# One transformer layer with mixture of experts on one core: the last batch's block results summed on TensorE, in place of a store and a gather by row

## What is computed

```python
x = x + attention(layernorm(x))              # 16 heads, causal softmax, projection wo
y = layernorm(x)                             # 4096 tokens x 128
shared = gelu(y @ Wfc_s + bfc_s) @ Wproj_s + bproj_s
p = softmax(y @ Wr); topk_p, topk_i = top_k(p, 2); topk_p /= sum(topk_p)
routed = sum over the two chosen e of topk_p[e] * (gelu(y @ Wfc[e] + bfc[e]) @ Wproj[e] + bproj[e])
x = x + shared + routed
```

## Time and profile before

| | |
|---|---|
| runs | 707.07, 712.68 and 709.67 us, median 709.67 us |
| the profiled execution | 714.72 us |
| its span, first to last instruction | 713.0 us |
| busy: PE, PEld | 592.3 us (83%), 442.1 us (62%) |
| busy: DVE, ACT, POOL | 411.3 us (58%), 402.4 us (56%), 328.7 us (46%) |
| mean granted TensorE clock | 0.941 |
| bytes moved by DMA | 100.99 MB, 142 GB/s over the span |

### The profile page before, as it was taken

How to read it: one execution, slowest core, us unless ns; L and a number is a source line. 1 busy time by engine, 2 the same in 40 slices (tenths; PEclk the granted TensorE clock), 3 DMA queues, 4 the chain that set the end, 5 groups by cost and what they waited for, 6 DMA issues and landing times.

```text
span 713.0 us, 15616 instructions
## 1 busy us (share of the span) xinstructions
PE 592.3 (83%) x5166; PEld 442.1 (62%) x5166; DVE 411.3 (58%) x1135; ACT 402.4 (56%) x723; POOL 328.7 (46%) x441
## 2 busy tenths in 40 slices
PE   2798599989999899998799969999978888857730
PEld 2565366546566566565478957888755676857620
DVE  7799378596788887987744434347643244322222
ACT  4255475556666666685465967795556735414210
POOL 6817142885673783764440141013237554242344
PEclk9799899999999999999999999999998999989875
DMA  5187878101001000102517693767752466768732
GB/s 164 31 258 204 236 244 271 58 16 39 22 4 27 27 10 16 30 20 73 185 31 229 210 278 123 242 218 247 244 183 68 127 216 213 245 184 275 240 98 59
DMA packets 64734, 100.99 MB, mean 142 GB/s; under 512 B 9276, under 2 KB 50016, under 8 KB 64224
## 3 DMA queue, kind: packets, MB, share of 16 engines
q1 hardware_dynamic: 60560, 91.60, 41.8%
q0 software_dynamic: 4096, 8.40, 3.8%
HBM read 83.89 MB, written 32.79 MB: 164 GB/s over the span
## 4 chain that ended last, share of the span: by engine, by line
PE 50%; DVE 18%; issue 13%; DMA 9%; ACT 5%; POOL 3%; another core or an unknown queue 1%; SPq 1%; POOLq 0%; DVEq 0%; ACTq 0%
DVE negmax L1007 10%; PE banks L1313 10%; PE banks L1392 7%; PE banks L1400 7%; PE banks L1295 6%; PE banks L1234 5%; PE banks L1283 5%; DMA xs<-x2n,row 5%; PE banks L1375 3%; PE banks L1370 3%; PE banks L1285 2%; ACT probs L873 2%; DMA got<-ys,from_row 2%; ACT hblk L911 1%; PE banks L1253 1%
## 5 line engine op out<-in xcount | busy, mean ns | idle before, releaser
L1007 DVE TENSOR_REDUCE negmax<-banks 128x2 f32<-128x768 f32 (+3 forms) x192 | 193.0, 1038 | 59.9 <-PE banks L1285 59.3
L873 ACT ACTIVATE probs<-banks 128x1024 f32<-128x1024 f32 (+2 forms) x192 | 157.4, 892 | 44.6 <-PE banks L1295 43.1
L911 ACT ACTIVATE hblk<-banks,wcur 128x128 f32<-128x128 f32 x340 | 95.6, 375 | 97.2 <-PE banks L1392 83.3
L770 POOL DMA_INDIRECT xs<-x2n,row x64 | 63.0, 985 | 157.0 <-DVE row L1091 73.3
L743 POOL TENSOR_SCALAR_AFFINE_SELECT probs<-probs 128x512 f32<-128x512 f32 x128 | 79.8, 640 | 117.5 <-ACT probs L873 116.1
L1283 PE MATMUL banks<-kpad,qst 128*128 128x256 bf16 (+3 forms) x512 | 118.3, 306 | 14.8 <-issue 8.8
L1392 PE MATMUL banks<-xblkT,wcur 128*128 128x128 f32 x680 | 98.0, 291 | 17.2 <-DVE yblk L1148 6.6
L1392 PEld LDWEIGHTS banks<-xblkT,wcur 128*128 128x128 f32 x680 | 88.9, 204 | 25.6 <-issue 11.1
L1400 PE MATMUL banks<-wcur,hblk 128*128 128x128 f32 x680 | 96.0, 288 | 5.9 <-ACT hblk L911 5.1
L1295 PE MATMUL banks<-qmst,kpad 128*128 128x512 bf16 (+3 forms) x512 | 93.3, 305 | 5.6 <-DVE negmax L1007 2.2
L1285 PE MATMUL banks<-future,identb 128*128 128x128 bf16 x512 | 97.0, 222 | 0.0
(11 more groups left out here) (142 smaller groups left out, 777.2 us busy)
## 6 DMA issues: line engine op xcount, KB each, us to landing
...
```

Source lines behind the costliest of these rows:

```text
L770: pool.indirect_dma_start(out=xs[g % 2], out_offset=bass.IndirectOffsetOnAxis(ap=row[:, b % 2, k, i:i + 1], axis=0), in_=x2n[:, b % NX2, i ...
L873: nc.scalar.activation(probs[:, g % 2, heads[0]:heads[-1] + 1, PCOL[tiles]:PCOL[tiles] + P * tiles], unit_view(PLACE["E", b, n], tiles), A ...
L911: ins = nc.scalar.activation(hblk[:, k % 3, q, :], one(PLACE["HB", g, s])[:, P * q:P * q + P], ACT.Gelu_apprx_tanh, bias=wcur[:, k % NW, 2 ...
L1007: dve.tensor_reduce(negmax[:, g, tiles - 1, heads[0]:heads[-1] + 1], unit_view(PLACE["M", b, n], tiles), AX.X, ALU.max, negate=True).then_ ...
```

## The change

For batch 7 alone (group 2) the results no longer pass through DRAM. Its YS and GA steps are gone, and `ys` has only two parts. In their place:

- SL.7 (`row_numbers`) leaves the row numbers as f32 in `compact`.
- DG (`spread_diagonals`) writes, on DVE, four sets of diagonal 128x128 matrices: row numbers for the first and the second expert, and the two weights. It is one memset of 128x128 and four operations of 128x512.
- RB, four steps (`spread_rows`), multiplies each set by a matrix of ones on PE, four matmuls a step; that spreads the numbers over all partitions. RE, four steps on ACT (`evacuate_rows`), copies them to SBUF, 128x512 each.
- SB, one step for each of the 15 blocks (`make_sums`): two DVE operations of 128x512, all in SBUF, that compare the row numbers with the block's rows and put the token's weight where they are equal. There are three places (`NSUM`).
- CM, one step a block (`add_up`): eight f32 matmuls, four token tiles by two experts, of these matrices with `yblk`. All 15 steps add up in one bank (7), which stays taken until CB.7 has read it.
- CB.7 (`combine_summed`) is now one addition of 128x256 a half, from PSUM.

All five tables are new throughout, the attention's steps too. The core of the diff:

```diff
-    GA.6.0 GA.6.1 GA.6.2 GA.7.0 GA.6.3 GA.7.1 GA.7.2 GA.7.3
+    GA.6.0 GA.6.1 GA.6.2 GA.6.3
...
-MORE = {"Y": NT, "YB": 2}
+LAST, LASTB = len(GROUPS) - 1, B - 1
+NSUM = 3
+MORE = {"Y": NT, "YB": 2, "CM": NBLK[LAST]}
...
-        ys = [dram(f"ys{g}", (NBLK[g] * P, C)) for g in range(len(GROUPS))]
+        ys = [dram(f"ys{g}", (NBLK[g] * P, C)) for g in range(LAST)]
...
+        block_row = sb("block_row", [P, NBLK[LAST]])
+        compact = sb("compact", [P, 2, NT])
+        spare = probs[:, 0].rearrange("p r w -> p (r w)")
+        onesf = xn[:, 0, :]
+        token_rows = spare[:, 0:4 * T].rearrange("p (n t) -> p n t", n=4)
+        diagonals = spare[:, 4 * T:8 * T].rearrange("p (n i c) -> p n i c", n=4, i=NT)
+        sums = spare[:, 4 * T:4 * T + 2 * NSUM * T].rearrange("p (n k t) -> p n k t", n=NSUM, k=2)
...
+        diag_ready, spread_done, token_rows_ready, sums_ready, summed = (
+            sem("diag_ready"), sem("spread_done"), sem("token_rows_ready"), sem("sums_ready"), sem("summed"))
...
-                if i > 0 and b < B - 1:
+                if i > 0:
...
+            pool.iota(block_row[:], pattern=[[P, NBLK[LAST]]], base=0, channel_multiplier=1, allow_small_or_imprecise_dtypes=True)
...
+            def evacuate_rows(n):
+                act.wait_ge(spread_done, nth("RB", LASTB, n))
+                copy(token_rows[:, n, :], one(PLACE["RB", LASTB, n])).then_inc(token_rows_ready, 1)
...
+                elif kind == "RE":
+                    evacuate_rows(n)
...
+                if b == LASTB:
+                    dve.tensor_tensor(compact[:], row_f[:, b], from_f[:], ALU.subtract).then_inc(from_ready, 1)
+                    return
...
+            def spread_diagonals():
+                dve.wait_ge(from_ready, nth("SL", LASTB))
+                dve.wait_ge(pv_done, nth("PV", LASTB, 2))
+                dve.wait_ge(xn_turned, nth("T1", LASTB))
+                dve.memset(onesf, 1.0)
+                eye = ident[:].unsqueeze(1).to_broadcast([P, NT, P])
+                for k in range(2):
+                    dve.tensor_tensor(diagonals[:, k], eye, bc(compact[:, k], P), ALU.mult)
+                for k in range(2):
+                    ins = dve.tensor_tensor(diagonals[:, 2 + k], eye, bc(wtop[:, LASTB, :, k], P), ALU.mult)
+                ins.then_inc(diag_ready, 1)
+            def make_sums(s):
+                dve.wait_ge(token_rows_ready, after("RE", LASTB, range(4)))
+                if s >= NSUM:
+                    dve.wait_ge(summed, nth("CM", LAST, s - NSUM))
+                for k in range(2):
+                    ins = dve.scalar_tensor_tensor(sums[:, s % NSUM, k, :], token_rows[:, k, :], block_row[:, s:s + 1],
+                                                   token_rows[:, 2 + k, :], ALU.is_equal, ALU.mult)
+                ins.then_inc(sums_ready, 1)
+            def combine_summed(h):
+                dve.wait_ge(summed, nth("CM", LAST, NBLK[LAST] - 1))
+                dve.wait_ge(acc_ready, nth("SA", LASTB))
+                at = slice(NT // 2 * h, NT // 2 * h + NT // 2)
+                dve.tensor_tensor(acc[:, LASTB, at], one(PLACE["CM", LAST, 0]).rearrange("p (i c) -> p i c", i=NT)[:, at],
+                                  acc[:, LASTB, at], ALU.add).then_inc(out_ready, 1)
...
-                    dve.wait_ge(y_stored[k % NY], 16 * (k // NY))
+                    pg, pp = pair_at(k - NY)
+                    if pg == LAST:
+                        dve.wait_ge(summed, after("CM", pg, range(2 * pp, 2 * pp + in_pair(pg, pp))))
+                    else:
+                        dve.wait_ge(y_stored[k % NY], 16 * (k // NY))
...
+                elif kind == "DG":
+                    spread_diagonals()
+                elif kind == "SB":
+                    make_sums(n)
+                elif kind == "CB" and b == LASTB:
+                    combine_summed(n)
...
+            def spread_rows(n, place):
+                pe.wait_ge(diag_ready, 1)
+                for i in range(NT):
+                    ins = mm(one(place)[:, P * i:P * i + P], onesf, diagonals[:, n, i, :], start=True, stop=True)
+                ins.then_inc(spread_done, 1)
+            def add_up(g, s, place):
+                k = pairs_up_to(g, s // 2)
+                pe.wait_ge(sums_ready, nth("SB", g, s))
+                pe.wait_ge(yblk_ready, nth("YE", g, s // 2))
+                for i in range(NT):
+                    for k2 in range(2):
+                        ins = mm(one(place)[:, C * i:C * i + C], sums[:, s % NSUM, k2, P * i:P * i + P], yblk[:, k % NY, s % 2, :],
+                                 start=(s == 0 and i == 0 and k2 == 0), stop=(s == NBLK[g] - 1 and k2 == 1), skip_group_check=True)
+                ins.then_inc(summed, 1)
...
+                elif kind == "RB":
+                    pe.wait_ge(token_rows_ready, nth("RE", b, n))
+                elif kind == "CM":
+                    pe.wait_ge(out_ready, after("CB", LASTB, range(2)))
...
+                elif kind == "RB":
+                    spread_rows(n, place)
+                elif kind == "CM":
+                    add_up(b, n, place)
```

349 lines of the change are left out of this document (176 added, 173 removed).

## The result

The changed kernel takes 686.96 us (median of 4 runs, 680.73 to 688.82), the kernel before 710.56 us in the same comparison: a ratio of 0.966, with a 95% interval of 0.959 to 0.972. That is 23.6 us less; forecast were 9.5 us less. The time lies under the predicted range of 690 to 711 us.

A forecast was written before the change was run, and what follows sets the result against it. The prediction took batch 7's gather queue, not PE, to set the end; gathers also held PE back. Tail 7.5 us less plus 2 elsewhere made 9.5: 709.67 - 9.5 = 700.2 us; own range 697 to 704, whole 690 to 711.

The forecast's parts named there:

- Elsewhere every table is new: Ahead of the tail: new orders cover some of PE's wait for group 1's rows, 2 us less (6.4 less to 6 more).
- The tail: End of the span, group 2 and batch 7: 705.5 instead of 713.0, 7.5 us less.
- the hoist: RC.7 no longer behind CB.2.1 and SL.4 on DVE: batch 7's first send 4.1 us earlier, bounds 0 and 4.6.
- Removal: Batch 7's four GA steps and two CBs go: last gather is GA.6.3, the store's end 704.1 instead of 713.0.
- The rows of group 2 follow: PE's first rows of group 2 come earlier with batch 7's sends: 632.10 becomes 628.0.
- CM steps at 1.79 us: PE, group 2: eight matmuls a step take 1.79 us, 15 steps 26.8; up to 53.6 at the low clock.
- chain (b): Batch 4's last gather, DVE's steps behind it, then PE with 11 CMs (19.7 us): ends latest, 700.1, plus 5.4 is 705.5.
- Rival 2: Tail and attention: most is hidden, gathers alone set the end, attention gains 6.4 us; about 690 us, chance 0.15.
- Rival 3: Attention: its new order gives back 4 to 6 us of the tail's 7.5 in new stops; 706 to 708, chance 0.27.
- Rival 1: PE from 632 us on: CMs lengthen its end and slow the kernel; 716.5 to 730 in median terms, chance 0.08.
- Rival 4: Batch 6's gathers land 4.6 us later, 704.6; changes nothing alone, counted with the forecast, no chance of its own.
- The wait between a gather and three weight loads: Batch 4's gather: without waiting for the loads it would land some 4 us sooner; the forecast kept the wait.

The follow-up runs named there:

- new_orders_only: The kernel before with the changed kernel's new orders, without the one-hot sums, batch 7's rows stored and fetched as before: 692.62 us, ratio 0.971.
- rows_earlier: The kernel before with RC.7 moved directly behind RT.7 on DVE, ahead of XV.1.7, CB.2.1 and SL.4: 708.63 us, ratio 0.998.
- half_products: The changed kernel with one of the two one-hot products per block and token tile, leaving out each token's second expert: 683.95 us, ratio 0.964.
- new_all_sends_at_once: The changed kernel, with GpSimd not waiting for one pair of row sends to land before issuing the next, in all batches: 665.34 us, ratio 0.942.

## Why the prediction was wrong

**The step that failed** is "Elsewhere every table is new": it looked at one place, the 6.42 us stop before XT.1.0, and put down 2 us, between 6.4 less and 6 more. Measured were 18 us between the medians, 15 to 26 by the ratio's interval, and the traces put all of them ahead of RK.7: 595.85 became 578.39 us in new_orders_only and 566.24 in the changed kernel. The prediction's own sign of being wrong, RK.7 more than 6 us from 596, came. At the one place it looked at nothing was gained: from RK.6 to XT.1.0 it is 33.0 us before and 33.5 in new_orders_only. What it could have done was to count, for each long transfer chain, the work that stands between its start and its end in both orders: behind RK.4 and ahead of XT.0.0, and from there to RK.7. The counts (2911 and 2747 records ahead of XT.0.0) come from the orders alone, and the earlier trace rows had shown 71 us in which PE was not busy up to RK.7 (596 less 525). The prediction passed over them with "busy 525 us, most of the time". Also, one stop was weighed by its own length; four kernels that removed such stops one by one show that its length is no measure of what it costs.

**The tail** was 7.5 us in the forecast, of which 4.1 for RC.7 and 3.4 for the sums. The sums alone, without the hoist of RC.7, gave 4.2 us between the medians and 5.4 us behind RK.7. With both, the traces say 4.5 us from RK.7 on. So the tail was put 3 us too high, and it is the hoist's part that no run shows. Term by term:

- Removal: the last gather no longer sets the end. Right: it is issued at 669.03, ahead of the last CM's end at 674.72.
- The hoist, 4.1 us: not shown. rows_earlier has it alone and doesn't get faster; new_orders_only has it and takes as long from RK.7 to the end as the kernel before. In the changed kernel XT.2.0 came 38.2 us behind RK.7, not 32, and directly behind PE's step before it, since PE did the RBs and blocks of group 1 in that time. "The rows of group 2 follow" was wrong there. Undoing the hoist did cost 5 us, but PE's stop of 6.23 us for the bank of the ranks came with it, a way that the forecast did not have.
- CM steps at 1.79 us: right. The granted clock was 0.95 from XT.2.0 to the last CM (0.86 in the blocks of group 2 before); behind the stop of 3.60 us at 615.36 eight records took 2.04 us, about twice their time, and in half_products the two half CMs behind a stop of 3.61 us took 3.75. The Trainium skill, page "TensorE: Matmul & The Clock Gate", section "HAM oscillation — how this bites in real kernels", says that a burst of matmuls behind a long wait for data starts at the low clock; these rows agree. The rule does not make the CMs such work: they follow on other steps at once, as the forecast had it.
- CMs on the path: chain (b) had 19.7 us of them on it. Of the 13.4 us that half_products removed some 3 came out, so most of them lie where PE would stop anyway. The chain that ended last was of (b)'s kind, over a gather, DVE and then PE, but by a gather of batch 5 and not batch 4's last.
- From XT.2.0 to the last CM 70.3 us, forecast 72.1; from there to the end 4.2 us, forecast 5.4. Near.
- SB operations 0.71 us each (0.69 forecast), and hidden.

**The rivals.** Rival 2 (most hidden, and the attention better by 6.4 us) pointed the right way, with too small a sum: its 690 us were the low end of the range, and the 13.0 us that it gave the tail were 4.5. Rival 3, that the new order gives 4 to 6 us back, had 0.27 and was the opposite of what came. Rival 1 fell with the CMs' clock and cover. Rival 4 changed nothing, as it said: CB.6.1 follows CB.7 without a wait.

**The wait between a gather and three weight loads.** The forecast kept 4 us for it. No run tried it alone. That gathers and sends land slowly while DMA moves 190 to 240 GB/s is in these traces; how much of a pair's 4 to 7 us is queueing and how much its own latency stays open.

**What stays open**: whether the order of RK.4 and XT.0.0 could be had in the old tables by themselves; what RC.7's place is worth by itself; and what the sums are worth once the sends go out at once (PE then has no stop over 1.3 us behind 568 us in new_all_sends_at_once).
